# One attention stage of a fused transformer kernel: the second group's unit moved one place back in the order, its inputs made in other units, and two heads scored in a pair

## The chip, the cores and the metric

The kernel runs on one core of one Trainium2 chip. The metric is the device time of one execution in microseconds (us). TensorE (PE) multiplies, VectorE (DVE) reduces and copies, ScalarE (ACT) applies functions and copies, GpSimd (POOL) gathers rows by indirect DMA.

## The reference

Sixteen images with N = 113 tokens of D = 192 features (36 patches and 77 text tokens) pass through two layers: embedding, attention, mixture of experts, a second attention, and a routed block. Only the second attention is touched by the change. Cut to what matters, with x the normalised tokens:

```python
def _L1_attn_ref(x, w_qkv, w_g0, w_g1, w_proj, b_proj):      # DIM 192, 8 heads of 24, 2 groups of 96
    qkv = (x @ w_qkv.T).reshape(B, N, 3, H, hd)
    attn = softmax(einsum('bhnd,bhmd->bhnm', q, k) * scale)
    origin = einsum('bhnm,bhmd->bhnd', attn, v)              # eight heads
    head_x = 0
    for i, w in enumerate([w_g0, w_g1]):                     # two groups, the second needs the first
        cur = xg[:, :, i] + head_x
        q2, k2, v2 = split(cur @ w.T)
        a2 = softmax(einsum('bnd,bmd->bnm', q2, k2) * scale)
        head_x = einsum('bnm,bmd->bnd', a2, v2)
        outputs.append(head_x + origin[:, :, i])
    return concatenate(outputs) @ w_proj.T + b_proj
```

## The kernel before

`attn1_phase` does this stage in four steps (`it` 0 to 3) of four images. In each step ten *units* go through one pipeline: the two groups "g0" and "g1" and the heads 0 to 7, in the order of the list `UNITS`. It was written out by hand:

```python
UNITS = ["g0", 0, 1, 2, 3, 4, "g1", 5, 6, 7]
```

A unit n passes: *scores* on PE into one of two PSUM banks (line 1664 for a group, 1666 for a head); `softmax_in` on DVE, which takes the maximum (1946) and subtracts it into SBUF (1950), after which the bank is free; the exponential on ACT (1832); `turn` on PE, the transposes (1685); the copy of the transposed tile on ACT (1854); and the product with the values on PE (1695 for a group, 1711 for four heads at once). A group is also normalised on DVE (`normalise`, 1958 to 1962) between the exponential and the turn.

Every engine runs a program of its own, a loop over n = 0 to 9 in which the pieces stand in a fixed order, and the engines meet at semaphores. Each engine takes its instructions strictly in that order, so that a wait holds up all that stands behind it. DVE and ACT work `AHEAD` = 2 units ahead of the turn: in place n, DVE does `softmax_in(n + 2)`. PE scores unit n + 2 in place n; in places 1 and 6 it scores units n + 2 and n + 3 together, as a pair, whose matmuls of 24 rows are issued alternately on different row groups of the array. `ready(it, n)` makes a score wait until the bank is free, that is until `softmax_in(n - 2)` is done; a pair waits for both.

The path of the two groups through a step, before:

- place 1, PE: `group_values` for g0 (1695), after `late_h`, which finishes the step before (1736, 1737). It waits until DVE has added the last product of `late_h` into H (1995).
- place 2, DVE: `softmax_in(4)`, then `first_result`, which makes `cur` (1968) and a copy (1969), then the statistics of the next step (`h_stat`, 240 and 243). In places 0 and 1 DVE adds eight gathered expert rows each into the next step's H (`mixed`, 233); the last step has none of this.
- place 3, PE: score of unit 5, the turn, then `second_group`: queries and keys of the second group from `cur` (1607) and, in the same function, its values (1612), which wait until ACT has copied the queries (1822). ACT does that copy after the exponential of unit 5.
- places 4 and 5, PE: scores of g1 and of head 5, one at a time; `values` of four heads in place 5.
- place 6: the pair of heads 6 and 7, `back` (1721), the turn of g1, then `pre_group`, the first projections of the next step (1607).
- places 7 and 8: `pre_qk`, the large projections of the next step (1628), and `group_values` for g1 in place 7.

In the last step the pieces of the next stage (`nxt.pre_z`, `pre_features` 1333 and 1334, `pre_router1` 1383 and 1384, `pre_mean` 1490 and 1492) stand in places 2 to 8.

Of the kernel before, what the change touches and what calls it, by code (L numbers as in the profile page):

```python
# [71 lines left out]
def done(s, it, n):  # L72


    return s.sem, s.per * (it + 1) + n + 1
# [1436 lines left out]
def attn1_phase(nc, dram, S):  # L1512
# [4 lines left out]
    HEADS, HD, GROUPS = 8, D // 8, 2  # L1517
    GD = D // GROUPS
    SCALE = float(HD) ** -0.5
    UNITS = ["g0", 0, 1, 2, 3, 4, "g1", 5, 6, 7]  # L1520
    NU = len(UNITS)
    HQ = 4
    NQ = HEADS // HQ
# [2 lines left out]
    with ExitStack() as ctx:  # L1526
# [60 lines left out]
        def _(pe):  # L1587
# [16 lines left out]
            def group_qk(it, tiles, n, i, x):  # L1604
                for m, c in ((n, 0), (n + 1, GD)):
                    pe.wait_ge(*tiles.free(it, m))
                    mm(tiles.bank(m)[0:GD, 0:GN], S.w1g[0:GD, i, c:c + GD], x[:], start=True, stop=True).then_inc(tiles.filled.sem, 1)
# [34 lines left out]
            def second_group(it):  # L1642

                pe.wait_ge(*group.copied(it, HX0))
                group_qk(it, group, GQ1, 1, cur)
                group_v(it, group, GV1, 1, cur)

            def ready(it, n):
# [101 lines left out]
            def body(it, first, last):  # L1750
                for n in range(NU):
                    if n == 0 and first:
                        scores(it, 2)
                    if n in (1, 6):
                        scores(it, n + 2, n + 3)
                    if n in (3, 4, 5):
                        scores(it, n + 2)
                    if n == 8 and not last:
                        scores(it + 1, 0)
                    if n == 9 and not last:  # L1760
                        scores(it + 1, 1, 2)
                    if n == 6:
                        back(it, 0)
                    turn(it, n)
                    if n == 0 and not first:
                        late_o(it - 1)
                    if n == 1 and not first:
                        late_h(it - 1)
                    if n == 3:
                        second_group(it)  # L1770
                    if n == 5 and not last:
                        pre_x(it + 1)
                    if n == 6 and not last:
                        pre_group(it + 1)
                    if n == 7 and not last:
                        pre_qk(it + 1, 0)
                    if n == 8 and not last:
                        pre_qk(it + 1, 1)
                    if n == 2 and last:
                        pe.wait_ge(*proj.copied(it, V1))  # L1780
                        pe.wait_ge(*proj.copied(it, GV0))
                        pe.wait_ge(S.early_ok, 2 * EARLY)
                        pe.wait_ge(S.late_in, 16 * len(S.late_loads))
                        pe.wait_ge(S.late_fill_ok, len(S.late_fill))
                        nxt.pre_z(0, False)
                    if n == 3 and last:
                        nxt.pre_features(0)
                    if n == 4 and last:
                        nxt.pre_router1(0)
                    if n == 5 and last:  # L1790
                        nxt.pre_router2(0)
                    if n in (6, 7, 8) and last:
                        nxt.pre_qk(0, n - 6)
                    if n in (1, 7):
                        group_values(it, n - 1)
                    if n == 5:
                        values(it, 1, 2, 3, 4)
                values(it, 5, 7, 8, 9)
                if not last:
                    pre_v(it + 1)  # L1800
                else:
                    nxt.pre_v(0)
                back(it, 1)
                if not last:
                    group_v(it + 1, proj, GV0, 0, xa)
# [8 lines left out]
        @block.scalar  # L1814
        def _(act):
            nxt = ffn1_pre_scalar(nc, act, S)
            credit(act, S.F.proj.outs["act"], proj.outs["act"], group.outs["act"], exp_ok, pt_out, ot_ok)
            cp = nc.scalar.activation

            def evac(it, tiles, n, out, rows_):  # L1820
                act.wait_ge(*done(tiles.filled, it, n))
                cp(out, tiles.bank(n)[0:rows_, 0:GN], ACT.Copy).then_inc(tiles.out(n), 1)

            def pre_v(it):
                act.wait_ge(*done(proj.filled, it, V1))
                cp(v[:, 2:4, :, 0:HD], proj.bank(V1)[0:N, 0:2 * D].rearrange("p (g h d) -> p g h d", g=2, h=HEADS), ACT.Copy
                   ).then_inc(proj.out(V1), 1)

            def exp(it, n):
                act.wait_ge(*units.copied(it, n))  # L1830
                pp = p[:, n % SLOTS, :, :]
                cp(pp, pp, ACT.Exp, scale=SCALE).then_inc(exp_ok.sem, 1)

            def outputs(it, g):

                act.wait_ge(*done(pv_ps, it, HQ * g + HQ - 1))
                act.wait_ge(*done(back_ps, it, g - 1))
                cp(ot[:], O[:, 0:GN], ACT.Copy).then_inc(ot_ok.sem, 1)

            def lead():  # L1840
                evac(0, proj, X1, xa[:], GD)
                evac(0, proj, GQ0, gq[:], GD)
                evac(0, proj, GK0, gk[:], GD)
                evac(0, proj, Q0, q[:, 0, :], 128)
                for n in range(AHEAD):
                    exp(0, n)
                evac(0, proj, Q1, q[:, 1, :], 128)
                pre_v(0)

            def body(it, first, last):  # L1850
                for n in range(NU):
                    act.wait_ge(*done(pt_ps, it, n))

                    cp(pT[:, n % 5, :, :], PT[0:N, 0:GN], ACT.Copy).then_inc(pt_out.sem, 1)  # L1854
                    if n + AHEAD < NU or not last:
                        exp(*unit(it, n + AHEAD))
                    if n == 3:
                        evac(it, group, GQ1, gq[:], GD)
                        evac(it, group, GK1, gk[:], GD)
                    if n == 5 and not last:  # L1860
                        evac(it + 1, proj, X1, xa[:], GD)
                    if n == 6 and not last:
                        evac(it + 1, proj, GQ0, gq[:], GD)
                        evac(it + 1, proj, GK0, gk[:], GD)
                    if n == 5:
                        outputs(it, 0)
                    if n == 7 and not last:
                        evac(it + 1, proj, Q0, q[:, 0, :], 128)
                    if n == 7:
                        evac(it, group, HX1, hx[:, 1, :], GD)  # L1870
                    if n == 8 and not last:
                        evac(it + 1, proj, Q1, q[:, 1, :], 128)
                    if n == 2 and last:
                        act.wait_ge(S.late_in, 16 * len(S.late_loads))
                        act.wait_ge(S.late_fill_ok, len(S.late_fill))
                        nxt.pre_z(0)
                    if n == 3 and last:
                        nxt.pre_features(0)
                    if n == 4 and last:
                        nxt.pre_router1(0)  # L1880
                    if n == 5 and last:
                        nxt.pre_router2(0)
                    if n in (6, 7, 8) and last:
                        nxt.pre_q(0, n - 6)
                outputs(it, 1)
                if not last:
                    pre_v(it + 1)
                else:
                    nxt.pre_v(0)

            steps(act, lead, body, lambda it: None)
# [22 lines left out]
        def _(dve):  # L1914
# [92 lines left out]

            def body(it, first, last):
                for n in range(NU):
                    if n + AHEAD < NU or not last:  # L2010
                        softmax_in(*unit(it, n + AHEAD))
                    if n == 0 and not first:
                        late_o(it - 1)
                    if n == 1 and not first:
                        late_h(it - 1)
                    if n == 2:
                        first_result(it)
                    if n in (0, 1) and not last:
                        mixed(nc, dve, S, it + 1, 2 * n)
                        mixed(nc, dve, S, it + 1, 2 * n + 1)  # L2020
# [2 lines left out]
                        h_stat(nc, dve, S, it + 1)  # L2023
                    if n == 4 and not last:
                        norm(it + 1)
                    if n == 3:
                        evac(it, group, GV1, gv[:], images(group.bank(GV1)[0:N, 0:G * GD]))
                    if n == 5 and not last:
                        pre_x(it + 1)
                    if n == 5:  # L2030
                        normalise(it, 1)
                    if n == 6:
                        divide(it, 0)
                    if n == 7 and not last:
                        pre_k(it + 1, 0)
# [858 lines left out]
```

## Time and profile before

| | |
|---|---|
| median of three runs | 1000.82 us (999.4 to 1003.1) |
| profiled execution, whole time | 1005.92 us |
| its span | 1004.2 us |
| PE busy | 827.9 us (82%) |
| DVE busy | 494.4 us (49%) |
| ACT busy | 307.0 us (31%) |
| POOL busy | 363.8 us (36%) |

The page gives the busy time of each engine, the chain of work that ended last, and the granted TensorE clock by slices. The trace behind it answers for single stretches: a timeline of one engine (start, duration, engine, line, operation, output and inputs; in brackets the idle time before it and what released it) and a table of windows with the busy time of each engine and the mean granted clock, where 1.00 is 2.4 GHz and 0.50 is 1.2 GHz. The attention stage in question runs from 436 to 653 us of the span.

### The profile page before, as it was taken

Reading aid. Unit: us, or ns where it says so; the run is one execution under the profiler, and the core shown is the slowest. Engines: PE = TensorE matmul, PEld = TensorE weight load, DVE = VectorE, ACT = ScalarE, POOL = GpSimd, SP = SyncE. Lnnn points to the kernel's source line nnn. Section 1 sums busy time; section 2 is a strip of 40 time slices with the busy share of each in tenths; the row PEclk is TensorE's granted clock in tenths of the full one; section 3 lists DMA queues with packets and bytes.
Section 4 is the critical chain, followed back from the end, with each engine's and each line's share of the span. In section 5 each row is a group of like instructions: output and inputs, shape, how many; then the busy total and the mean of one; then the engine's idle time right before and its main releaser. Section 6 shows DMA issues by size and latency. Waiting matters only on the chain.

```text
span 1004.2 us, 14809 instructions
## 1 busy us (share of the span) xinstructions
PE 827.9 (82%) x4860; PEld 596.0 (59%) x4860; DVE 494.4 (49%) x1223; ACT 307.0 (31%) x571; POOL 363.8 (36%) x233
## 2 busy tenths in 40 slices
PE   7998883189899999989979798868799799978571
PEld 4665662156567777767767665554656656647351
DVE  4345654434534455757575854364743652643310
ACT  1112421023233333323323335334343243342110
POOL 3015888787800387678784000010100010000000
PEclk9677765579989999995979696957879969989795
DMA  8811113334433344452110000000000000000000
GB/s 230 273 61 43 36 31 73 75 76 121 112 104 91 87 115 116 97 169 48 31 33 20 1 1 1 1 2 0 1 1 1 12 2 0 9 6 1 14 0 14
DMA packets 81395, 52.96 MB, mean 53 GB/s; under 512 B 42942, under 2 KB 76719, under 8 KB 80305
## 3 DMA queue, kind: packets, MB, share of 16 engines
q1 hardware_dynamic: 25026, 28.25, 9.8%
q0 software_dynamic: 40960, 11.98, 6.6%
q10 hardware_dynamic: 15344, 11.87, 4.1%
q8 instruction: 39, 0.64, 0.3%
q14 instruction: 26, 0.21, 0.1%
HBM read 29.53 MB, written 21.69 MB: 51 GB/s over the span
## 4 chain that ended last, share of the span: by engine, by line
PE 68%; DVE 11%; POOL 8%; issue 5%; ACT 3%; DMA 2%; SPq 0%; DVEq 0%; ACTq 0%; POOLq 0%
PE ex_up L1138 6%; POOL xs_scratch L209 6%; PE ex_up L1139 6%; PE ps L2264 4%; PE ps L2195 3%; PE ex_yp L1161 3%; PE ex_yp L1162 3%; PE ps L1628 3%; PE ps L1352 2%; PE ps L1354 2%; PE ps L1347 2%; PE ps L1666 2%; PE ps L1353 2%; PE ps L2204 2%; PE ps L1685 2%
## 5 line engine op out<-in xcount | busy, mean ns | idle before, releaser
L220 POOL DMA_INDIRECT work<-ys_scratch,place x64 | 152.8, 2387 | 93.2 <-DMA ys_scratch<-ex_yb 62.6
L209 POOL DMA_INDIRECT xs_scratch<-e_t,e_routed x64 | 152.3, 2379 | 41.4 <-issue 29.3
L1239 DVE TENSOR_SCALAR ex_bb<-ex_up 128x384 f32<-128x384 f32 x44 | 24.5, 558 | 123.4 <-PE ex_up L1139 99.9
L1138 PE MATMUL ex_up<-e_wa,ex_x 128*128 x176 | 76.2, 515 | 11.0 <-issue 9.9
L1139 PE MATMUL ex_up<-e_wb,e_ex_x 65*128 x176 | 74.2, 503 | 0.0
L2474 POOL TENSOR_TENSOR H<-H,f_hh 113x768 f32 (+1 forms) x4 | 7.2, 1808 | 146.8 <-DVE f_hh L2617 146.8
L2452 POOL TENSOR_SCALAR f_veps<-f_mv 113x4 f32<-113x4 f32 x10 | 1.9, 193 | 144.2 <-DVE f_mv L2514 144.2
L2400 ACT ACTIVATE f_pT<-ps 113x452 f32<-113x452 f32 x48 | 26.2, 546 | 78.1 <-PE ps L2204 78.1
L1139 PEld LDWEIGHTS ex_up<-e_wb,e_ex_x 65*128 65x128 f32 x176 | 34.7, 197 | 25.1 <-issue 3.0
L1138 PEld LDWEIGHTS ex_up<-e_wa,ex_x 128*128 128x128 f32 x176 | 31.1, 196 | 29.2 <-issue 16.4
L1196 ACT ACTIVATE ex_sg<-ex_up 128x384 f32<-128x384 f32 x44 | 21.6, 490 | 87.0 <-PE ex_up L1139 86.9
L2195 PE MATMUL ps<-f_k,f_q 16*113 16x113 f32 x384 | 32.5, 320 | 16.3 <-DVE f_p L2554 15.3
L1161 PE MATMUL ex_yp<-e_wa,ex_a 128*128 x176 | 43.9, 331 | 0.8 <-ACT ex_yb L1203 0.8
L1162 PE MATMUL ex_yp<-e_wb,e_ex_a 65*128 x176 | 43.5, 328 | 0.0
L2195 PEld LDWEIGHTS ps<-f_k,f_q 16*113 16x113 f32 x384 | 27.5, 221 | 21.4 <-DVE f_p L2554 15.1
L1854 ACT ACTIVATE a_pT<-ps 113x452 f32<-113x452 f32 x40 | 21.8, 545 | 58.7 <-PE ps L1685 58.6
L2204 PE MATMUL ps<-ident,f_p 113*113 113x113 f32 x192 | 36.7, 324 | 3.6 <-ACT f_pT L2400 3.6
L2617 DVE SCALAR_TENSOR_TENSOR f_hh<-ps,f_bits,f_hh 113x192 f32<-113x192 f32 x16 | 5.9, 413 | 64.4 <-PE ps L2264 64.4
L2375 ACT ACTIVATE f_p<-f_p 113x452 f32<-113x452 f32 x48 | 27.7, 578 | 32.3 <-DVE f_p L2554 31.8
L1121 PE MATMUL ex_xt<-ident,ex_xb 128*128 128x128 f32 x88 | 22.7, 283 | 17.7 <-DMA ex_xb<-xs_scratch 17.7
L1203 ACT ACTIVATE ex_yb<-ex_yp 128x384 f32<-128x384 f32 x44 | 21.6, 490 | 50.3 <-issue 26.6
L2264 PE MATMUL ps<-fc,f_ff 128*113 128x192 f32 x192 | 36.8, 344 | 0.0
(372 smaller groups left out, 1986.6 us busy)
## 6 DMA issues: line engine op xcount, KB each, us to landing
ex_xb<-xs_scratch SPq DMA_DIRECT2D x88, 96.0 KB, 5.3
ys_scratch<-ex_yb ACTq DMA_DIRECT2D x44, 192.0 KB, 5.2
e_wa<-in_wa SPq DMA_DIRECT2D x4, 1152.0 KB
xs_scratch<-e_zeros SPq DMA_DIRECT2D x46, 96.0 KB, 4.2
e_wb<-in_wb SPq DMA_DIRECT2D x4, 576.0 KB
e_wa<-in_patches SPq DMA_DIRECT2D x4, 432.0 KB, 9.7
xs_scratch<-e_zeros ACTq DMA_DIRECT2D x16, 96.0 KB, 5.8
out<-H SPq DMA_DIRECT2D x4, 339.0 KB
```

The lines of the kernel that those rows point to most:

```text
L209: nc.gpsimd.indirect_dma_start(out=dram.xs, out_offset=bass.IndirectOffsetOnAxis(ap=S.pos[:, j, k:k + 1], axis=0), in_=S.t[:, j, :], in_of ...
L220: nc.gpsimd.indirect_dma_start(out=S.yk[:, it % 2, j, k, :], out_offset=None, in_=dram.ys[it // X.steps], in_offset=bass.IndirectOffsetOnA ...
L1138: mm(o, x1[:, p % 3, t], S.wa[:, bass.ds(w, 2 * I)], start=True, stop=False)
L1139: m = mm(o, x2[:, p % 3, t], S.wb[:, bass.ds(w, 2 * I)], start=False, stop=True)
L1161: mm(o, a1[:, p % 2, t], S.wa[:, bass.ds(w, D)], start=True, stop=False)
L1162: m = mm(o, a2[:, p % 2, t], S.wb[:, bass.ds(w, D)], start=False, stop=True)
L1628: m = mm(proj.bank(n)[:, 0:GN], S.w1w[0:GD, i, col + 128 * t:col + 128 * (t + 1)], x[:], start=(i == 0), stop=(i == 1))
L2195: m = mm(units.bank(h)[0:N, s], q[r:r + HD, h // HQ, s], k[r:r + HD, h // HQ, s], start=True, stop=True, tile_position=(r, 0))
L2204: m = nc.tensor.transpose(PT[0:N, j * N:(j + 1) * N], p[:, n % (AHEAD + 1), j, :], S.ident[0:N, 0:N])
L2264: m = mm(o, ff[:, f, j * N:(j + 1) * N], S.fc2[:, f, :], start=False, stop=(f == KF - 1))
L2375: cp(pp, pp, ACT.Exp, scale=float(HD) ** -0.5).then_inc(exp_ok.sem, 1)
L2400: cp(pT[:, n % 5, :, :], PT[0:N, 0:GN], ACT.Copy).then_inc(pt_out.sem, 1)
```

## The change

The unit g1 goes from place 6 to place 7 of the order, behind head 5. Heads 4 and 5 (units 5 and 6) are scored as a pair in place 3, and g1 alone in place 5. The product of g0 with its values goes from place 1 to place 2, that of g1 from 7 to 8. On DVE `first_result` stands in front of `softmax_in(4)`. The values of the second group become a function of their own, `second_values`, issued in place 4 of PE and copied in place 4 of DVE; the copy of the g1 result goes to place 8 on ACT, `normalise(it, 1)` to place 6 on DVE. No work is added or taken away.

```diff
-    UNITS = ["g0", 0, 1, 2, 3, 4, "g1", 5, 6, 7]
+    UNITS = ["g0", 0, 1, 2, 3, 4, 5, "g1", 6, 7]
...  (PE)
                 group_qk(it, group, GQ1, 1, cur)
+
+            def second_values(it):
                 group_v(it, group, GV1, 1, cur)
...
-                    if n in (1, 6):
+                    if n in (1, 3, 6):
                         scores(it, n + 2, n + 3)
-                    if n in (3, 4, 5):
+                    if n == 5:
                         scores(it, n + 2)
...
                     if n == 3:
                         second_group(it)
+                    if n == 4:
+                        second_values(it)
...
-                    if n in (1, 7):
-                        group_values(it, n - 1)
+                    if n in (2, 8):
+                        group_values(it, {2: 0, 8: 7}[n])
                     if n == 5:
                         values(it, 1, 2, 3, 4)
-                values(it, 5, 7, 8, 9)
+                values(it, 5, 6, 8, 9)
...  (ACT)
-                    if n == 7:
+                    if n == 8:
                         evac(it, group, HX1, hx[:, 1, :], GD)
...  (DVE)
+                    if n == 2:
+                        first_result(it)
                     if n + AHEAD < NU or not last:
                         softmax_in(*unit(it, n + AHEAD))
...
-                    if n == 2:
-                        first_result(it)
...
-                    if n == 3:
+                    if n == 4:
                         evac(it, group, GV1, gv[:], images(group.bank(GV1)[0:N, 0:G * GD]))
...
-                    if n == 5:
+                    if n == 6:
                         normalise(it, 1)
-                    if n == 6:
                         divide(it, 0)
```

## Rows read from the trace of the kernel before

**Rows 1.** The page: the span, and the chain that ended last by engine.

```profile
span 1004.2 us, 14809 instructions
...
PE 68%; DVE 11%; POOL 8%; issue 5%; ACT 3%; DMA 2%; SPq 0%; DVEq 0%; ACTq 0%; POOLq 0%
```

**Rows 2.** Timeline of PE in the second step, 504 to 530 us.

```profile
505.74 0.99 PE L1695 MATMUL ps<-a_pT,a_gv 113*96 113x113 f32 x8 [1.58 <-DVE H L1995]
...
507.05 1.04 PE L1666 MATMUL ps<-a_k,a_q 24*113 24x113 f32 x8
...
510.54 1.76 PE L1607 MATMUL ps<-a_cur,w1g 96*96 96x452 f32 x4 [1.87 <-DVE a_hx L1969]
514.22 1.83 PE L1612 MATMUL ps<-w1g,a_cur 96*113 96x96 f32 x8 [1.92 <-ACT a_gq L1822]
...
517.39 0.97 PE L1685 MATMUL ps<-ident,a_p 113*113 113x113 f32 x4
518.29 1.86 PE L1666 MATMUL ps<-a_k,a_q 24*113 24x113 f32 x8
...
524.28 1.87 PE L1666 MATMUL ps<-a_k,a_q 24*113 24x113 f32 x16
...
527.82 2.46 PE L1607 MATMUL ps<-a_xa,w1g 96*96 96x452 f32 x4
```

**Rows 3.** Timeline of DVE in the second step, 505 to 511 us.

```profile
505.51 2.71 DVE L233 SCALAR_TENSOR_TENSOR H<-work,shares,H 113x192 f32<-113x192 f32 x8
...
508.79 0.63 DVE L1950 TENSOR_TENSOR a_p<-ps,a_mx 113x452 f32<-113x452 f32 x1
509.34 0.61 DVE L1968 TENSOR_TENSOR a_cur<-ps,a_xb 96x452 f32<-96x452 f32 x1
509.87 0.61 DVE L1969 COPY a_hx<-ps 96x452 f32<-96x452 f32 x1
```

**Rows 4.** Windows: length, busy times of five engines, granted clock, DMA share, GB/s.

```profile
480.00:485.00 5.00, 5.00 (x15) 2.49 (x14) 1.08 (x2) 3.31 (x7) 4.62 (x2) 0.84 0.20 37
...
510.00:515.00 5.00, 2.54 (x8) 1.35 (x9) 3.05 (x11) 1.92 (x5) 4.31 (x5) 0.73 0.19 34
...
525.00:530.00 5.00, 5.00 (x25) 3.56 (x23) 3.14 (x6) 1.50 (x4) 4.39 (x3) 0.56 0.20 36
...
560.00:565.00 5.00, 3.19 (x15) 2.74 (x15) 1.69 (x3) 1.44 (x3) 1.24 (x2) 0.51 0.00 0
...
580.00:585.00 5.00, 5.00 (x27) 3.23 (x26) 1.64 (x5) 1.99 (x4) 0.00 (x0) 0.94 0.00 0
...
610.00:615.00 5.00, 5.00 (x20) 3.04 (x19) 0.84 (x2) 1.70 (x2) 0.00 (x0) 0.63 0.01 3
...
630.00:635.00 5.00, 4.67 (x15) 2.12 (x14) 1.67 (x4) 3.54 (x5) 0.00 (x0) 0.82 0.00 0
```

**Rows 5.** Timeline of PE in the first and in the third step.

```profile
462.23 3.33 PE L1607 MATMUL ps<-a_cur,w1g 96*96 96x452 f32 x4 [1.25 <-DVE a_hx L1969]
465.91 1.84 PE L1612 MATMUL ps<-w1g,a_cur 96*113 96x96 f32 x8 [0.35 <-ACT a_gq L1822]
...
479.51 0.96 PE L1607 MATMUL ps<-a_xa,w1g 96*96 96x452 f32 x1
...
558.59 1.87 PE L1607 MATMUL ps<-a_cur,w1g 96*96 96x452 f32 x4 [1.87 <-DVE a_hx L1969]
...
575.87 3.22 PE L1607 MATMUL ps<-a_xa,w1g 96*96 96x452 f32 x4
```

**Rows 6.** Timelines of PE and DVE in the last step.

```profile
602.54 0.99 PE L1695 MATMUL ps<-a_pT,a_gv 113*96 113x113 f32 x8 [0.74 <-DVE H L1995]
...
604.63 1.04 PE L1666 MATMUL ps<-a_k,a_q 24*113 24x113 f32 x8
...
616.79 1.87 PE L1383 MATMUL ps<-f_e,ro 128*128 128x452 f32 x2 [1.35 <-DVE f_gs L1492]
...
615.92 0.61 DVE L1490 TENSOR_REDUCE f_gm<-f_e 128x4 f32<-128x448 f32 x1
```

## The prediction

> **What bounds the kernel now.** I read the page first: PE carries 68% of the chain that ended last, DVE 11% [rows 1]. So the question is what keeps PE from working in this stage. The timeline of PE in the second step answers it [rows 2]; the other steps repeat it [rows 5, 6]. Behind `late_h` PE stands three times: 1.58 us before the values of g0 (DVE's add into H), 1.87 before `second_group` (DVE's `first_result`), 1.92 before the second group's values (ACT's copy of the queries). From there to the projections of the next step at 527.82 it has no pause.
>
> The windows give the other half of the cost [rows 4]. A clock of 0.73 over 510 to 515 us puts the fall from 2.4 to 1.2 GHz at 512.3; 0.56 over 525 to 530 puts the return at 529.4. PE had paused twice before the fall, and was busy without a break for 15.2 us before the return. The other returns are at 481.6, 580.6 and 631.8, the other falls shown at 560.1 and 611.3. Each return lies in the large projections: 2.1, 1.6 and 4.7 us behind the start of `pre_group` (479.51, 527.82, 575.87). At 1.2 GHz the work costs about double: `second_group` takes 3.33 us in step one and 1.76 in step two [rows 5, 2].
>
> DVE sets the times around this. It works through `mixed` from 505.51, `softmax_in(4)` until 509.4, then `first_result` until 510.5 [rows 3]. The reader is to see that these follow one another without a gap: whatever is put ahead of something there delays it.
>
> **The change part by part.**
>
> *The pair.* A single head's score takes 1.86 us at the low clock, the pair of two heads 1.87 [rows 2]: the second head is free. Start to start these are 1.79 and 1.80. The pair of heads 4 and 5 thus saves one score: 1.79 where it stood (unit 7), or the 1.04 of unit 5 at the full clock.
>
> *What the pair waits for.* Unit 5 alone needed `softmax_in(3)`. The pair also needs the bank of unit 6, so `softmax_in(4)`, and DVE now does `first_result` before that. The DVE work is the same, only swapped, so `softmax_in(4)` ends where `first_result` ended, at 510.5, and the pair starts at 510.6. Ahead of it PE has only the turn of unit 2 and the values of g0. The turn moves into the first pause (half a us of 1.58); the values still wait for DVE's add, start at 505.74 and end near 506.6. So PE stands from 506.6 to 510.6, 4.0 us, where it stood 1.87. Behind the pair in PE's queue are the turn of unit 3 and `second_group`, whose input `cur` is ready already at 508.7: it waits for the pair, not for its own data. A pause of 4.0 us is longer than either after which the clock fell before, so I take the clock as low from before 510.6.
>
> *The second group's values* go behind the turn of unit 4. The copy of the queries is then done: ACT's exponential of unit 5 follows DVE's subtraction near 513.8, the copy ends by 515.7, the values come at 517.4. The pause of 1.92 goes (0.35 in step one). This is hidden by the low clock's long `second_group`; at the full clock it is still covered, within 0.3 us.
>
> *Sum for step two*, from the start of the stalled work to `pre_group`. Before: 510.54 to 527.82, 17.28 us. Now: less the pause 1.92, less the single score 1.79, plus the pair 1.80, plus the turn of unit 3 at 0.90 (517.39 to 518.29), plus 1.5 because `second_group` runs at the low clock (3.33 for 1.76). That is 17.8; from 510.6 it ends at 528.4, 0.6 later. Step one was at the low clock already: from 462.3, 17.28 less 0.35, less 1.79, plus 1.80, plus 0.90 is 17.8, and the end moves from 479.51 to 480.1, 0.6 later. Step three: 558.7 plus 17.28 less 1.8, less 1.79, plus 1.80, 0.90 and 1.4 gives 576.5 for 575.87, 0.6 later. Together 1.8 us slower.
>
> *The last step* has no `mixed`. PE ends `late_h` at 601.8. The turn, `pre_z` and the values of g0 took 2.09 us (602.54 to 604.63) [rows 6] and end near 603.9, now in one piece. DVE's `first_result` and `softmax_in(4)` take 1.1 and 1.3 us, two operations each [rows 3], so the pair starts at 606.5, after a pause of 2.6 us that was not there. If the clock falls in it: pair 1.8, turn 0.9, `second_group` 3.2, `pre_features` 3.3 (two pairs like those of the router, 1.87 overlapping), turn 0.9, values of the group 1.6, which ends at 618.2. Only then can DVE copy these values (0.6), and only behind that copy stands `pre_mean`, 0.87 us to the router [rows 6]; with two wake-ups `pre_router1` starts at 619.9 instead of 616.79. This is a new queueing: the mean waits behind a copy of something else. Afterwards g1 (1.54) is scored where a head was (1.79), so the step ends 2.9 later. If the clock falls only after the pair and the turn, 1.7. I take 2.3. If it does not fall at all, see below.
>
> *Edits I cost at nothing.* `group_values` of g1 behind `pre_qk` of place 8: it is moved past busy PE work. ACT's copy of it now stands ahead of a copy of queries, which has 1 us of scores to hide it. `normalise` one place later: 1.5 us on DVE, covered by `back`, the turn and `pre_group` on PE (about 5 us at the low clock); if PE ran at the full clock there it would have 0.5 us to spare. No DMA is issued by any moved piece; the gathers of POOL feed `mixed`, which keeps its place.
>
> **Sum.** 1.8 + 2.3 = 4.1 us slower against the profiled 1005.92, so 1010.0 there. The runs shown have their median 5.1 below the profiled time; the same difference on the median gives 1004.9 us. What a measurement of this kernel can tell from no change is about 0.5%, 5 us.
>
> **The rivals.**
>
> *A, the full clock comes back sooner.* If unbroken work brings it back, not the large projections, the 15.2 us of step two count from 510.6 and end at 525.8, not at 530.0 (1.6 behind the new `pre_group`); half of the 4.2 us is saved. Step one: 15.7 us from 462.3, 478.0 for 482.2, 2.1. Step three: 18.3 us, 2.1. Together 6.3: 1005 less 6.3 is 998.6. For it: three of the four last pauses are followed by a return after 15 to 16 us. Against: each return also coincides with large projections. It cannot be told apart from this trace.
>
> The Trainium skill (TensorE: Matmul & The Clock Gate, "What's actually happening") says "the default state is throttled, and activity releases the throttle", which would have the return soon after the 4.0 us pause, and by it three steps would run 19 us each at double pace, near 976 us. Rows 4 speak against: 15.2 us of unbroken busy work ran at 0.50. I give this extreme 1 in 100.
>
> *B, the full clock comes back later (the slower side).* In step three the return was 4.7 us behind the start of `pre_group`, in step two 1.6 [rows 4, 5]. Where a return slips by these 3.1 us against the work, half is lost, 1.6. Two or three of four such slips give 1008 to 1010. It decides from two slips on.
>
> *C, the last step keeps the full clock (the faster side).* Its pause is 2.6 us, short of 4.0, and in the last step before it there was no fall behind pauses of 0.7 each. Then `second_group`, `pre_features` and the turn run at 2.4 GHz, the values no longer wait for ACT, and the router starts at 614.1 instead of 616.79, 2.7 sooner; the 15.0 us from there to the return at 631.8 were at the low clock and lose up to 7.5, of which I give back 2 for ACT, which has an exponential and a table for the router to do in between. The step is 8 us shorter instead of 2.3 longer: 994.6. It decides if the clock stays at 1.00 over 606 to 611. Against: PE does only a little small work between 604 and 608.
>
> *D, the pair's wait is shorter than worked out*, because DVE gets through `mixed` sooner. Nothing in the rows lets it; it would give 1001.
>
> **Chances.** The forecast 0.50 (own range 1001 to 1008), A 0.15, B 0.24, C 0.07, D 0.03, the extreme 0.01. Faster by over 0.5%: C and the lowest of A, 0.09. Slower by over 0.5%: B without its edge, and a third of the forecast's case, 0.38. Within: 0.53. The range takes in A and B: 997 to 1010.
>
> **What would show it.** In PE's timeline: a pause of about 4.0 us in front of the first x16 pair behind the values of g0 in steps one to three, released by L1950, and of 2.6 in the last; no pause before L1612; L1607 from `cur` at 3.3 us; `pre_group` 0.6 us later against the step's start. In DVE's: in the last step `f_gm` behind `a_gv`. The prediction is wrong if the pair starts by 508, if the granted clock over 510 to 515 is above 0.8, or if the returns move against `pre_group`.

## The result, and the profile after

The changed kernel takes 984.0 us (median of four executions, 980.8 to 989.3) where the one before takes 1002.0 (four, 999.4 to 1003.6). The ratio is 0.9846, with a 95% interval of 0.9806 to 0.9887: it is 1.5% faster, where 0.4% slower was forecast, and the time lies outside the range of 997 to 1010. The two medians alone give 0.982, inside the interval. The profiled execution took 989.3 us. Some executions of any of these kernels are some per cent slower than the others at a lower mean clock; ratios and medians below leave them out.

The page of the changed kernel: span, PE's busy time, the chain by engine.

```profile
span 987.6 us, 14813 instructions
...
PE 809.7 (82%) x4860; PEld 580.6 (59%) x4860; DVE 495.7 (50%) x1223; ACT 306.8 (31%) x571; POOL 365.1 (37%) x233
...
PE 64%; DVE 12%; POOL 11%; issue 6%; ACT 3%; DMA 1%; SPq 0%; DVEq 0%; ACTq 0%; POOLq 0%
```

PE issues the same 4860 matmuls, yet is busy for 18 us less: the mean granted clock over the span is 0.842 where it was 0.832. PE's timeline in the second step answers to [rows 2]:

```profile
496.52 0.99 PE L1697 MATMUL ps<-a_pT,a_gv 113*96 113x113 f32 x8 [1.19 <-ACT a_pT L1858]
501.42 1.86 PE L1668 MATMUL ps<-a_k,a_q 24*113 24x113 f32 x16 [3.91 <-DVE a_p L1954]
503.22 1.10 PE L1687 MATMUL ps<-ident,a_p 113*113 113x113 f32 x4
504.11 3.22 PE L1607 MATMUL ps<-a_cur,w1g 96*96 96x452 f32 x4
507.12 0.96 PE L1687 MATMUL ps<-ident,a_p 113*113 113x113 f32 x4
507.88 1.70 PE L1612 MATMUL ps<-w1g,a_cur 96*113 96x96 f32 x8
509.37 1.76 PE L1666 MATMUL ps<-a_gk,a_gq 96*113 96x113 f32 x8
...
513.46 0.69 PE L1600 MATMUL ps<-ident,n_x 113*96 113x113 f32 x5 [1.01 <-DVE n_x L259]
...
518.35 3.22 PE L1607 MATMUL ps<-a_xa,w1g 96*96 96x452 f32 x4
```

The pause in front of the pair is there, 3.91 us for the 4.0 worked out, released by the subtraction of `softmax_in(4)` (line 1954 now). `second_group` runs at the low clock, 3.22 us. The pause in front of L1612 is gone. All of this is the schedule as forecast for this step. The same lines of PE in steps one, three and four, which answer to [rows 5, 6]:

```profile
459.25 1.86 PE L1668 MATMUL ps<-a_k,a_q 24*113 24x113 f32 x16 [2.90 <-DVE a_p L1954]
...
461.94 3.00 PE L1607 MATMUL ps<-a_cur,w1g 96*96 96x452 f32 x4
...
465.17 0.94 PE L1612 MATMUL ps<-w1g,a_cur 96*113 96x96 f32 x8
...
470.84 1.68 PE L1607 MATMUL ps<-a_xa,w1g 96*96 96x452 f32 x4
...
550.53 1.86 PE L1668 MATMUL ps<-a_k,a_q 24*113 24x113 f32 x16 [3.91 <-DVE a_p L1954]
...
553.22 3.22 PE L1607 MATMUL ps<-a_cur,w1g 96*96 96x452 f32 x4
...
563.51 1.68 PE L1607 MATMUL ps<-a_xa,w1g 96*96 96x452 f32 x4
...
592.06 1.05 PE L1668 MATMUL ps<-a_k,a_q 24*113 24x113 f32 x16 [2.54 <-DVE a_p L1954]
...
593.52 2.45 PE L1607 MATMUL ps<-a_cur,w1g 96*96 96x452 f32 x4
...
601.30 1.88 PE L1383 MATMUL ps<-f_e,ro 128*128 128x452 f32 x2 [1.38 <-DVE f_gs L1492]
```

The reader is to see L1612 at 465.17 with 0.94 us: directly behind `second_group` the clock is already high again. The windows (columns as in [rows 4]) say when:

```profile
450.00:455.00 5.00, 3.77 (x26) 3.36 (x27) 4.97 (x14) 2.02 (x5) 4.39 (x3) 0.59 0.23 40
...
460.00:465.00 5.00, 5.00 (x23) 3.11 (x22) 4.34 (x12) 1.58 (x4) 3.73 (x3) 0.54 0.09 23
...
495.00:500.00 5.00, 1.33 (x12) 0.98 (x10) 5.00 (x14) 1.01 (x2) 4.39 (x3) 0.87 0.16 23
...
510.00:515.00 5.00, 3.99 (x50) 3.28 (x49) 4.18 (x8) 0.55 (x1) 4.47 (x3) 0.76 0.15 28
...
555.00:560.00 5.00, 5.00 (x46) 3.93 (x49) 3.15 (x14) 2.62 (x5) 0.04 (x1) 0.82 0.01 3
```

A clock of 0.59 over 450 to 455 us is a fall at 450.9, before the long pause of step one, and 0.54 over 460 to 465 is a return at 464.6, 5.3 us after PE resumed at 459.25. In step two the clock falls at 498.7, inside the long pause, and returns at 512.4, 11 us after it; in step three it falls at 549.9, in the pause, and returns at 556.8, 6.3 us after it. In the last step the pair still runs at the full clock, 1.05 us, and the clock falls only inside `second_group`, at 594.3. Before, 15 to 18 us had passed between the last pause and the return. In the stage the low clock held for 48 us in all, where it held for 85 before; the stage (first group score to the last product of `late_h`) took 193.7 us for 210.3. The difference of 16.6 us is that of the spans. Outside the stage the two executions differ by 3.1 us one way and 3.1 the other.

One pause is new, 1.01 us in front of the next step's transposes in step two. It comes from POOL, here with DVE's normalisation that waited for it:

```profile
510.78 2.63 DVE L259 TENSOR_SCALAR n_x<-H,n_mv,n_rstd 113x192 f32<-113x192 f32 x4 [5.00 <-POOL n_rstd L251]
```

```profile
504.21 2.37 POOL L220 DMA_INDIRECT work<-ys_scratch,place  x1 [0.30 <-issue]
506.88 2.37 POOL L220 DMA_INDIRECT work<-ys_scratch,place  x1 [0.30 <-issue]
509.32 0.19 POOL L249 TENSOR_SCALAR n_veps<-n_mv 113x4 f32<-113x4 f32 x1
```

The statistics were ready at 502.7, but POOL had gathers queued in front of the root. After this pause the clock fell once more, from 515.8 to 522.6.

### The profile page after: what moved, and what is told of

It reads as the page before. It is cut to its first block, busy times and chain, and to the rows that moved or that the text cites. A ratio compares the mean times of both kernels' runs of the same rounds, so it can differ in the third digit from the quotient of the medians.

```text
span 987.6 us, 14813 instructions
## 1 busy us (share of the span) xinstructions
PE 809.7 (82%) x4860; PEld 580.6 (59%) x4860; DVE 495.7 (50%) x1223; ACT 306.8 (31%) x571; POOL 365.1 (37%) x233
## 4 chain that ended last, share of the span: by engine, by line
PE 64%; DVE 12%; POOL 11%; issue 6%; ACT 3%; DMA 1%; SPq 0%; DVEq 0%; ACTq 0%; POOLq 0%
PE ex_up L1138 6%; PE ex_up L1139 6%; POOL xs_scratch L209 5%; POOL work L220 4%; PE ps L2267 3%; PE ps L2198 3%; PE ex_yp L1161 3%; PE ex_yp L1162 3%; PE ps L1347 2%; PE ps L1354 2%; PE ps L1352 2%; PE ps L1628 2%; PE ps L2207 2%; PE ps L1353 2%; PE a_ps L389 1%
## 5 line engine op out<-in xcount | busy, mean ns | idle before, releaser
L1138 PEld LDWEIGHTS ex_up<-e_wa,ex_x 128*128 128x128 f32 x176 | 31.2, 196 | 26.3 <-issue 13.7
L2207 PEld LDWEIGHTS ps<-ident,f_p 113*113 113x113 f32 x192 | 29.7, 226 | 12.5 <-issue 10.9
L2553 DVE TENSOR_REDUCE f_mx<-ps 113x4 f32<-113x452 f32 x48 | 29.9, 623 | 12.4 <-PE ps L2198 11.4
```

The lines of the kernel that those rows point to most:

```text
L1138: mm(o, x1[:, p % 3, t], S.wa[:, bass.ds(w, 2 * I)], start=True, stop=False)
L2207: m = nc.tensor.transpose(PT[0:N, j * N:(j + 1) * N], p[:, n % (AHEAD + 1), j, :], S.ident[0:N, 0:N])
L2553: nv.tensor_reduce(mx[:, n % 2, :], sc, AX.X, ALU.max).then_inc(mx_ok.sem, 1)
```

## The experiments

Theory 1, formed on this result: the change gains through the clock alone, and what brings the clock back is work of PE that nothing interrupts. Before, `second_group` stood between two pauses, and the unbroken work began only behind the second; now it runs through from the pair on. Rivals: the pair brings the gain (theory 2), or one long pause is better than several short ones (theory 3).

All ratios are to the kernel before, with 95% intervals. "Low" is the time at 1.2 GHz in the whole execution, worked out as 2 x (1 - mean clock) x span and taken as the median; "rest" is the median of span x mean clock, what the execution would last if all work of the low time ran at double pace. The kernel before has low 321 to 326 and rest 835 to 836 in the three sets of runs. A pause that lies in low time counts half in "rest". "Stage" is the low time inside the attention stage, read from the windows of the one profiled execution; in the kernel before it is 85. The ratios are those on record; ratios of the plain medians differ from them by up to 0.004.

| kernel | ratio | interval | low | rest | stage |
|---|---|---|---|---|---|
| changed | 0.9846 | 0.9806 to 0.9887 | 295 | 835 | 48 |
| changed, again | 0.9855 | 0.9746 to 0.9964 | 297 | 837 | 44 |
| values at once | 0.9895 | 0.9846 to 0.9945 | 309 | 831 | 61 |
| single scores | 0.9859 | 0.9778 to 0.9940 | 296 | 832 | 58 |
| softmax first | 0.9842 | 0.9791 to 0.9893 | 291 | 837 | 44 |
| before, only values later | 0.9938 | 0.9887 to 0.9990 | 311 | 836 | 65 |
| pause put back | 1.0004 | 0.9961 to 1.0047 | 316 | 837 | 72 |
| pause filled | 0.9870 | 0.9789 to 0.9951 | 286 | 845 | 21 |
| before, filled | 0.9895 | 0.9854 to 0.9936 | 267 | 850 | 34 |
| before, no break | 0.9901 | 0.9856 to 0.9947 | 307 | 837 | 61 |
| next input later | 0.9872 | 0.9791 to 0.9952 | 309 | 833 | 58 |
| pause elsewhere | 0.9938 | 0.9892 to 0.9984 | 295 | 841 | 55 |
| filled and later | 0.9848 | 0.9764 to 0.9933 | 270 | 847 | 27 |

The first line shows where the change's time went: rest is what it was, low is 24 to 31 us shorter. Half of that is 12 to 15 us, for a gain of some 15.

The second set of executions of the changed kernel shows how far the same program varies. Its windows (PE resumed at 457.30 in step one and at 589.72 in the last):

```profile
465.00:470.00 5.00, 5.00 (x51) 4.70 (x54) 2.44 (x4) 1.57 (x4) 4.39 (x3) 0.56 0.19 37
...
590.00:595.00 5.00, 5.00 (x33) 2.73 (x29) 4.04 (x7) 3.92 (x8) 0.00 (x0) 1.00 0.01 3
595.00:600.00 5.00, 3.62 (x25) 2.68 (x24) 1.32 (x4) 4.94 (x6) 0.00 (x0) 1.00 0.00 0
```

In step one the clock came back at 469.4, 12.1 us after PE resumed, where the first profile has 5.3; in steps two and three it took 11.1 and 6.9. In the last step it did not fall at all. Single steps of one program thus differ by 7 us of low time, and small differences in the column "stage" can be chance.

**The parts of the change, one undone at a time.**

```diff
                     if n == 3:
                         second_group(it)
-                    if n == 4:
                         second_values(it)
```

> The changed kernel with the second group's values issued right behind its queries and keys again (place 3 of PE), everything else as changed. Theory 1 (unbroken work): the clock comes back early because second_group is no longer followed by a pause before L1612; here that pause of 1 to 2 us is back, so the low stretches are long again (17 us or more each, over 70 us in the four steps together, where the changed kernel has 48) and the time is 994 to 1003. Theory 2 (fuller work): the pair takes the poorly filled single scores out of the stretch, and that brings the clock back; then this run stays at 982 to 989, since its scores are the same. Theory 3 (one long pause in place of three short ones is cheaper by itself): also 982 to 989.

It lies between, 0.9895, and its premise failed. PE's timeline in its second step:

```profile
506.90 3.22 PE L1607 MATMUL ps<-a_cur,w1g 96*96 96x452 f32 x4
509.91 1.70 PE L1612 MATMUL ps<-w1g,a_cur 96*113 96x96 f32 x8
```

There is no pause in front of L1612, although the values stand right behind. The exponential that ACT does before copying the queries is done in time here, since the pair had scored unit 5 before `second_group`. So this kernel doesn't have the break that it was made for, and is no test of theory 1; its low stretches in the stage were 13.7 us in three steps and 20.5 in the first.

```diff
-                    if n in (1, 3, 6):
+                    if n in (1, 6):
                         scores(it, n + 2, n + 3)
-                    if n == 5:
+                    if n in (3, 4, 5):
```

> The changed kernel with units 5, 6 and 7 scored one by one in places 3, 4 and 5, everything else as changed. Unit 5 then waits only for softmax_in(3), so the 3.9 us pause in front of it goes and a shorter one (about 1.3 us) stands in front of second_group; one more score of 1.0 to 1.8 us per step. Theory 1 (unbroken work behind second_group): 980 to 988. Theory 2 (the pair's fuller work brings the clock back): 994 to 1003. Theory 3 (one long pause is better than short ones): above 990.

0.9859: without the pair the gain is there, to within the intervals. As the main cause, theory 2 falls.

```diff
-                    if n == 2:
-                        first_result(it)
                     if n + AHEAD < NU or not last:
                         softmax_in(*unit(it, n + AHEAD))
+                    if n == 2:
+                        first_result(it)
```

> The changed kernel with softmax_in(4) in front of first_result on DVE, as before the change. The pair can start 1.1 us sooner (a pause near 2.8 us instead of 3.9), second_group finds its input just ready. Theory 1: the clock falls and returns as in the changed kernel, 979 to 986. Theory 3 (it is the length of the one pause that matters): long low stretches again, above 990.

0.9842: the long pause is a us shorter (2.84 us), the time the same. With the run before, in which it is 1.06, theory 3 falls.

This is the kernel before with one part of the change:

```diff
                 group_qk(it, group, GQ1, 1, cur)
+
+            def second_values(it):
                 group_v(it, group, GV1, 1, cur)
...
+                    if n == 4:
+                        second_values(it)
...  (DVE)
-                    if n == 3:
+                    if n == 4:
                         evac(it, group, GV1, gv[:], images(group.bank(GV1)[0:N, 0:G * GD]))
```

> The kernel before, with one part of the change alone: the second group's values go behind the turn of unit 4 on PE (and their copy to place 4 on DVE). Order of units, scores and first_result as before. Theory 1: most of the gain, 984 to 992, low stretches of 13 us or less in steps one to three, and no pause in front of L1612 in the steps in which g1 is scored later. But g1 is scored at the head of place 4 here, in front of the moved values, and it needs the keys' copy, so that a pause of up to 2 us may stand in front of L1664 instead; if so, 996 to 1002. Theory 2: no gain, 997 to 1002.

0.9938. Behind `second_group`, in front of g1's score, stood a pause of 0.78 us in steps one and two and of 2.35 in step three, as the expectation allowed for; low is 311, two fifths of the way.

**Putting the break back, and taking only the break away.** First the changed kernel with a wait:

```diff
             def second_values(it):
+                pe.wait_ge(*done(exp_ok, it, 6))
                 group_v(it, group, GV1, 1, cur)
```

> The changed kernel with a wait put in front of the second group's values: PE waits there for the exponential of unit 6, a pause of about 1.3 us behind second_group and the turn of unit 4; no work changed. Theory 1 (the clock returns early because nothing breaks the work behind the long pause): the low stretches grow to those of the kernel before (17 us and more a step), time 993 to 1003, ratio about 0.995. Rival (only the amount of work between matters, a pause of 1 us does not): 4 pauses of 1.3 us, 985 to 990.

PE's timeline in steps one and two, and a window of each:

```profile
468.47 1.83 PE L1612 MATMUL ps<-w1g,a_cur 96*113 96x96 f32 x8 [1.10 <-ACT a_p L1837]
...
511.01 3.22 PE L1607 MATMUL ps<-a_cur,w1g 96*96 96x452 f32 x4
514.02 0.96 PE L1688 MATMUL ps<-ident,a_p 113*113 113x113 f32 x4
516.09 1.83 PE L1612 MATMUL ps<-w1g,a_cur 96*113 96x96 f32 x8 [1.10 <-ACT a_p L1837]
```

```profile
475.00:480.00 5.00, 4.75 (x51) 3.12 (x41) 2.96 (x7) 2.54 (x5) 4.41 (x2) 0.90 0.20 36
...
515.00:520.00 5.00, 3.91 (x20) 3.91 (x21) 1.37 (x3) 1.02 (x2) 4.39 (x3) 0.50 0.17 25
```

A pause of 1.10 us behind `second_group` (2.53 in the last step) takes the gain: 1.0004 (0.998 by the plain medians). Low rises by about 20 us, rest by 2 at most. The time is what theory 1 gave. The low stretches did not grow as it said in every step: they were 23.9, 13.7, 17.1 and 17.1 us, 72 together, where the kernel before has 85, and low stays 10 below that kernel's. Behind the pause the clock was back after 7.5, 4.3 and 6.0 us, not after 15 to 18. Now the kernel before, with the later values of the last run above and g1 scored behind them:

```diff
-                    if n in (3, 4, 5):
+                    if n in (3, 5):
                         scores(it, n + 2)
...
                     if n == 4:
+                        second_values(it)
+                        scores(it, 6)
```

> The kernel before with the second group's values behind the turn of unit 4, and g1 scored behind them: nothing but the break behind second_group is taken away. Scores are single, unit order, first_result and the values of g0 as before; the pause of 1.87 us in front of second_group stays. Theory 1: low stretches of 14 us or less in most steps, 984 to 991, nearly all of the change's gain. Rival (the pair, or g1 later in the order, brings the gain): 997 to 1003.

0.9901, nearly two thirds of the gain and just short of what theory 1 gave, with the order of units, the single scores, `first_result` and the values of g0 of the kernel before. The low stretches were 6.8, 27.3, 17.1 and 10.2 us. In step two PE waited 3.07 and 1.24 us for the next step's normalised rows while the clock was low. The break itself was not taken away everywhere; in step three a piece is left:

```profile
548.81 1.83 PE L1607 MATMUL ps<-a_cur,w1g 96*96 96x452 f32 x4 [1.87 <-DVE a_hx L1974]
552.49 1.83 PE L1612 MATMUL ps<-w1g,a_cur 96*113 96x96 f32 x8 [1.09 <-ACT a_gq L1827]
```

`second_group` had begun at the full clock, took 1.8 us and was through before ACT had the queries out. In step two of the changed kernel, where the long pause brings the clock down, `second_group` is slow enough (3.22 us) to cover that copy.

```diff
                     if n == 8 and not last:
+                        pe.wait_ge(*done(exp_ok, it + 1, 0))
                         pre_qk(it + 1, 1)
```

> A control for the pause put back behind second_group: the changed kernel with a wait of about the same length (1 to 1.7 us) in another place, between the large projections of the next step (place 8, for the exponential of the next step's first unit), in steps one to three. Theory 1 says that only a break in the low stretch costs more than itself: here 3 pauses cost 3 to 5 us and the low time stays, 985 to 991. Rival (any pause of this kind costs 3 to 4 us each through the clock): 995 to 1000.

The control, on the changed kernel: pauses that add up to the same (1.60, 1.60 and 2.50 us for 1.10, 1.10, 1.10 and 2.53), but where the clock is high. PE's timeline and windows in step two, and in step three:

```profile
521.46 1.02 PE L1628 MATMUL ps<-a_xa,w1w 96*128 96x452 f32 x2 [1.60 <-ACT a_p L1837]
```

```profile
515.00:520.00 5.00, 4.86 (x25) 3.15 (x24) 2.88 (x6) 2.29 (x6) 4.39 (x3) 1.00 0.19 37
520.00:525.00 5.00, 3.54 (x13) 2.00 (x14) 0.96 (x3) 1.02 (x2) 4.39 (x3) 1.00 0.19 36
```

```profile
567.45 1.22 PE L1628 MATMUL ps<-a_xa,w1w 96*128 96x452 f32 x2 [2.50 <-ACT a_p L1837]
```

```profile
565.00:570.00 5.00, 2.55 (x5) 1.18 (x6) 1.75 (x5) 1.11 (x2) 0.00 (x0) 0.81 0.00 0
570.00:575.00 5.00, 4.78 (x33) 3.13 (x31) 1.36 (x3) 1.16 (x3) 0.00 (x0) 0.84 0.00 0
```

In step two the clock stays at 1.00 through the pause; behind the longer one of step three it fell too, for 3.4 us. Low is 295, as in the changed kernel; rest is 4 to 7 us more, about what the three pauses add up to (5.7 us). By the ratio the cost is larger: 0.0083 to 0.0092, 8 to 9 us. Behind `second_group` 5.8 us of pauses cost 0.0149 to 0.0158, some 15 us. The two kernels part clearly in low time, 311 to 345 us in the eight executions of the one and 284 to 316 in the nine of the other; the intervals of their ratios overlap a little.

**Filling the pauses.** `fill` issues matmuls of 96x96x452 whose results are overwritten; first in the changed kernel, then in the one before.

```diff
+                    if n == 3:
+                        pe.wait_ge(*group.free(it, GQ1))
+                        fill(it, group.bank(GQ1), 2 if last else 4)
                     if n in (1, 3, 6):
                         scores(it, n + 2, n + 3)
```

> The changed kernel with matmuls of no use in the pause in front of the pair: four of 96x96x452 (3.3 us) in steps one to three, two in the last, into a bank that second_group overwrites afterwards. If this pause is what makes the clock fall, the four low stretches go, or all but one, the stage loses up to 24 us: 962 to 975. If the clock falls for another reason (thin work of transposes and scores as such), 980 to 990.

0.9870. In the stage of its profile the low time was 21 us instead of 48, with no fall in the filled pause in any step. But the time did not follow: it missed the 962 to 975 forecast for that, low over the whole execution is only 8 to 11 us shorter and rest 7 to 10 more. PE's timeline in step two:

```profile
508.19 3.20 PE L1644 MATMUL ps<-a_xa,w1g 96*96 96x452 f32 x8
512.26 1.05 PE L1672 MATMUL ps<-a_k,a_q 24*113 24x113 f32 x16 [0.87 <-DVE a_p L1961]
...
522.13 0.91 PE L1600 MATMUL ps<-ident,n_x 113*96 113x113 f32 x3 [4.05 <-DVE n_x L259]
```

At the full clock PE is early for the next step's normalised rows, and waits 4 us for DVE, which waits for POOL.

```diff
             def second_group(it):
+                pe.wait_ge(*group.free(it, GQ1))
+                fill(it, group.bank(GQ1), 2)
                 pe.wait_ge(*group.copied(it, HX0))
                 group_qk(it, group, GQ1, 1, cur)
+                pe.wait_ge(*done(pt_out, it, 3))
+                fill(it, PT, 2)
                 group_v(it, group, GV1, 1, cur)
```

> The kernel before with matmuls of no use in two of its three pauses: two in front of second_group and two in front of the second group's values, where PE stood 1.87 and 1.92 us; nothing of the change. Theory 1 (the change gains through the clock alone): the low stretches of 85 us in the stage go for the most part, 965 to 980, as fast as the changed kernel or faster, though no order was changed. Rival (the change gains by its pairing or order itself): 995 to 1003.

0.9895: the kernel before, in its own order, gains 1% from matmuls that compute nothing. Low falls by 58 us against the kernel before, the largest fall here, and rest rises by 14: each fill took 3.2 us at the low clock and 1.7 at the full one (step one), where step one of the kernel before had pauses of 1.25 and 0.35 us, and a wait of 0.53 and 1.37 us for the rows turns up behind them in step two. Forecast was 965 to 980 by theory 1 and 995 to 1003 by its rival; the median is 987, between the two. That low time can be turned into a gain without any change of order is shown, the size was missed.

```diff
-                    if n == 5 and not last:           # PE; later in the same way on ACT and DVE
-                        pre_x(it + 1)
+                    if n == 6 and not last:           # behind scores(8, 9), ahead of back
+                        pre_x(it + 1)
```

> The changed kernel with the next step's first transposes (pre_x) one stretch later: on PE behind values and the pair of place 6, on ACT behind the copy of the head results, on DVE behind softmax_in(8). With the clock back early, PE otherwise waits there for the normalised rows (1.01 us in step two of the changed kernel, 5.7 us with softmax_in(4) first), and breaks the clock again. Theory 1: the second low stretch of step two goes, 976 to 985. Rival (that wait only moves to pre_group, which needs the copies of these transposes at once): 982 to 990.

> The changed kernel with the pause in front of the pair filled (four and two matmuls of no use) and pre_x later as in the other run. If what ate the gain of filling was the wait for the normalised rows that followed (4.05 us in step two there), it is shorter here: 970 to 980. If the fill's gain is bounded by DVE's and POOL's chain to the next step's rows, the wait turns up in front of pre_group: 984 to 992.

> The changed kernel once more, as the base of the comparisons, in more executions: 981 to 990, ratio 0.98 to 0.99; low time in the stage near 50 us.

The transposes one stretch later alone bring nothing (0.9872 and a low time of 309, where theory 1 had given 976 to 985 us; in step two PE waited 1.67 us for `softmax_in(7)` instead, which DVE does behind the normalisation). With the fill the ratio is 0.9848, the same as the changed kernel's. Its low time is 27 us shorter than that of the changed kernel's second set, and its rest 9 to 12 longer, and the 970 to 980 forecast was missed: in step two PE stood for 5.67 us in front of the next pair, behind DVE, which had waited 5.68 us for POOL's root. This wait bounds step two; that it bounds the whole was not tried. No version here is clearly faster than the changed kernel, which measured 0.9855 the second time.

## Why the prediction was wrong

**Right.** The swap on DVE delays the pair, and PE pauses for 3.91 us for 4.0 in steps two and three, 2.54 for 2.6 in the last. In steps two and three the clock falls in that pause, and the pair and `second_group` run at the low clock. In step one it had fallen before, as in the kernel before. In the last step it had not: the pair ran at the full clock and the fall came behind it, the branch to which the prediction gave 1.7 us. The pause in front of L1612 goes, also in the last step, where `f_gm` came directly behind the copy of `a_gv` as worked out, and PE waited 1.38 us for it. No wait of more than 0.5 us turned up in the stage's timeline at the edits costed at nothing.

**The step that failed** is the one behind the sums: the assumption that the clock stays low until the projections of the next step. I took "each return lies in the large projections" [rows 4, 5] for the place of the return in the new order too. That it stood there before was no sign of a cause. In the changed kernel the clock was back after 5.3, 11.0 and 6.3 us of unbroken work, before any projection of the next step, and the low time in the stage was 48 us for 85; this was also one of the signs that the prediction had named for being wrong, returns that move against `pre_group`. Taking `pre_group` against the turn of unit 0, step one was 5.6 us shorter and step three 4.2, where 0.6 longer was forecast for each; only step two, with its second fall, came out near (0.3 shorter). With the last step, 5.5 shorter for 2.3 longer, this is 15.6 of the stage's 16.6 us.

**Rival A** had the mechanism, unbroken work, and got 0.15; it was mis-sized, since it carried over the 15 to 18 us of the rows of before, which gave 998.6. Those counts began behind a pause, with thin work (single scores, transposes) in front. That the same number does not hold for other work was not considered. The measured 984.0 lies between A and the extreme of 976 that had 1 in 100.

The Trainium skill (TensorE: Matmul & The Clock Gate, "What's actually happening") calls the throttled state the default, which activity releases. I held the 15.2 us at 0.50 against it. In the changed kernel the trace is nearer to the page: the clock was back after 5.3 us of activity in step one of one execution, but after 12.1 in the same step of the other. The kernel before, with 15.2 us at 0.50, shows that not all busy time does so.

**Rival C** did not hold in the first profile: in the last step the clock fell as well, at 594.3, but returned at 597.7, and again from 601.1 to 604.5, and the step was 5.5 us shorter (from the first turn of the step, at 581.22, to the end of `late_h`: 52.1 us for 57.6). In the second profile its condition was met, with a clock of 1.00 from 590 to 610 us, and the step was 8.5 us shorter, where C had given 8. So it came true in one of two profiles. Rivals B and D had nothing.

**Shown and not shown.** Shown: the gain is clock time (low 24 to 31 us shorter at the same rest); pauses of 1.1 us behind `second_group`, and 2.5 in the last step, undo it; the pair and the place of `first_result` are not needed for it. Not shown is what exactly brings the clock back. Unbroken work is not the whole of it: 15 to 18 us of it ran at the low clock in the kernel before, and 4.3 to 7.5 were enough behind the pause put back. The rival that nobody tried is that the kind of work in that stretch counts as well as its length. Open are also what share the order of g1 and the values of g0 have in the last third, between 0.9901 and 0.9846, whose intervals overlap; and why the kernel with the values at once, which has no break in its profile, was at 0.9895.

## What to carry to other kernels

Price a pause of PE by what it does to the clock, not by its length: 5.8 us of waiting cost some 15 us behind `second_group`, where the clock was still low in most steps, and the same sum between the large projections, at the full clock, 4 to 9. The length of the wait in front (3.91, 2.84 or 1.06 us) made no difference that these runs could tell; a wait of 1.1 us behind it did. Take more than one profile before reading a length off one: the same program gave 5.3 and 12.1 us in the same step. And a place where the clock always returns in a trace is not yet its cause; ask what PE had done, and how long without a break, when it came.

## What the runs showed of the hardware

- With the clock low, the return came after 5.3 to 6.3 us of unbroken work in two steps of the changed kernel and after 11 in a third, in its second profile after 12.1, 6.9 and 11.1; in the kernel before, 15 to 18 us of it had passed in each of the four steps. Length of unbroken work alone does not set it. What kind of work counts was not tried.
- Short pauses were enough in front of a fall: in the kernel before, the last pause that ended ahead of each of the four falls took 0.90, 1.87, 1.87 and 1.62 us (falls at 454.3, 512.3, 560.1 and 611.3).
- The pair of two heads on different row groups took the time of one at both clocks: 1.05 us for 1.04 at the full clock (592.06 above, [rows 2]), 1.86 for 1.86 at the low one.
- Work that computes nothing can pay: with useless matmuls in two pauses the kernel before was 1% faster (0.9895).
